# Two-layer recurrent model, one core: the first attention's maxima two heads at a time and evenly spaced between its scores, keys and values of the next layer in the score banks, and one written list behind it

## The chip, the cores and the metric

The kernel runs on one core of one Trainium2 chip. The metric is the device time of one execution in microseconds (us), the median of several runs. TensorE (PE) multiplies, VectorE (DVE), ScalarE (ACT) and GpSimd (POOL) work on elements, SyncE (SP) issues the transfers.

## The reference

```python
x = L0_attn_x                       # 1 x 1024 x 512, float32
xn = _layernorm(x)
s = _L0_attn_ref(xn, ...)           # 1024 tokens, 8 heads of width 8
g = _silu(_L0_ffn_ref(xn, ...))     # base 512x512, plus top-2 of 8 experts of rank 16
x = x + s * g
xn = _layernorm(x)
s = _L1_attn_ref(xn, ...)           # 32 query heads, 8 key/value heads of 128, rms-normed q and k, ALiBi, causal
g = _silu(_L1_ffn_ref(xn, ...))     # NF4 weights 1376x512 plus rank 16
x = x + s * g
```

In `_L0_attn_ref` the shapes come from the input, so it is attention of all 1024 tokens over all 1024 tokens, 8 heads of width 8, with biases in the projections. `_L1_attn_ref` is causal over 1024 tokens. All matrices are float32; the kernel multiplies each as a high and a low part, so that one product is three matmuls (`mm3`).

## The kernel before, in words

The 1024 tokens are `NT` = 8 blocks of 128, `D` = 512 is `KT` = 4 slices of 128. Each engine has its own program; semaphores tie them, and nothing but the order in which each program is written sets the order of the work. PSUM has eight banks: `T[0]` and `T[1]` (a ring of two), `S[0]` and `S[1]` (two banks each, scores), `VB`, `WB`.

**Front.** Layer norm, projections `qk`, values and router `var`, and from these the maxima of the scores of half unit 0: `max0(x)` for x = 0 to 15 (4 blocks of queries times 4 heads). PE writes 128x1024 scores of one head to `S[x % 2]` (L1936), DVE takes the maximum (L1430) into `MX`. PE may start `max0(x)` when the maximum x - 2 is done. Between them stand the other `qk`, and DVE computes the routing (`RT`, `CMP`, L1449 to L1488), from which POOL makes the expert weights `HN` (L905).

**First attention.** 32 steps x (`NBX`), that is 4 units u (two groups of 4 heads by two halves of queries) times 8 blocks of keys. `unit_items(x)` lists a step for all engines: `("ST", 0)`, `("ST", 1)` are the transposed scores of heads 0, 1 and of heads 2, 3 (`keys0`, L2021; each matmul uses the 32 rows of its head), exponentiated by ACT (L1095); `("PV", x-1)` are the values of the step before (`values0`, L2032, four column strips). In the steps up to 23, `("MM", u, j)` is one of 16 pairs of maxima of the next unit: two heads' scores into both banks of the ring `T` (`max1` on PE, L2005), two reductions on DVE (L1506). A pair may start when both banks are free. Pairs with even j use heads 2, 3 and so fit beside `("ST", 0)`, odd j beside `("ST", 1)`. `FILL` holds what runs between: `("B", t, kt)` the base product of a token block into `WB`, `("X", t)` the transposed `HN`, `("HN", t)` the experts' product, after which ACT empties `WB` (L1144). `("SH", u)` transposes the shifts into the ring and DVE adds them (L1992, L1520). From step 24 the first four blocks go on (`token_items`): `OS` sums transposed, DVE `normalise`, `OH` transposed heads, `WO` output product, DVE gate (L1561), POOL adds x (`add_x`, L943), `LS` statistics, POOL `rstd` (L845, L846), `LA` normalisation on DVE (L1361), `XT` transpose, ACT and DVE high and low parts.

**Tail.** Behind the last values stand `TAIL` = `tail_items(0)` to `tail_items(11)`: the same for blocks 4 to 7, and for the second layer keys and values of the eight blocks (`KV`, into the ring `T`; ACT squares L1206 and the high part of the values L1208; DVE copies L1662, L1663), POOL's inverse root (L867, L868), the scaling `SC` (L1669), the transposed keys `KT` (L2144, L1181, L1640), queries `PQ` into `WB` with `SQ` and `QT`, and the first scores `S0`. After the list 64 slots of the second layer follow, which the change leaves as they are.

Of the kernel before, what the change touches and what calls it, by code (L numbers as in the profile page):

```python
# [102 lines left out]
for _x in ([("F", t) for t in range(NT)] + [("WO", t) for t in range(EARLY)] + [("PQ", 0)] + [("WO", t) for t in range(EARLY, NT)] + [("PQ", 1)]):  # L103
# [35 lines left out]
def unit_items(x):  # L139

    maxima = [[pair(2 * x + PAIRS_PRE + i)] if 2 * x + PAIRS_PRE + i < 3 * PAIRS else [] for i in range(2)]
    a, b = (min(n, FILL_X) * len(FILL) // FILL_X for n in (x, x + 1))
    fill = FILL[a:b] + head_items(x - EARLY_X)
    seq = [("ST", 0)] + maxima[0]
    if x:
        seq.append(("PV", x - 1))
    if x in (7, 15, 23):
        seq.append(("SH", x // NT + 1))
    return seq + [("ST", 1)] + maxima[1] + fill
# [116 lines left out]
KV_STEP = (0, 0, 1, 2, 6, 7, 8, 10)  # L266
SC_STEP = (1, 1, 2, 3, 7, 8, 9, 11)
KT_STEP = (2, 3, 4, 5, 8, 9, 10, 11)
TAIL_STEPS = 12


def tail_items(k):


    seq = [("XT", EARLY - 1), ("KV", 0), ("PQ", 0)] if k == 0 else []
    seq += token_items(EARLY + k, EARLY, NT)
    if k == 9:
        seq.append(("PQ", 1))
    seq += [("SC", b) for b in range(NT) if SC_STEP[b] == k]
    if k == 11:  # L280
        seq.append(("SQ", 1))
    seq += [("KT", b) for b in range(NT) if KT_STEP[b] == k]
    seq += [("KV", b) for b in range(1, NT) if KV_STEP[b] == k]
    return seq + {1: [("SQ", 0)], 2: [("QT", 0)], 11: [("S0", 0), ("QT", 1)]}.get(k, [])


TAIL = [x for k in range(TAIL_STEPS) for x in tail_items(k)]
T_AT = {}
for _x in TAIL:
    if _x[0] in ("OS", "OH", "XT", "KT", "KV", "QT"):  # L290
        T_AT[_x] = T_OUT + len(T_AT)
# [124 lines left out]
def program(nc, x, w0, w1, codes, absmax, lora, consts, rows, rel, out):  # L416
    with ExitStack() as ctx:
# [36 lines left out]
        RSTD = sb("RSTD", [P, 2])  # L454
        SQK = sb("SQK", [P, 3, 8])
# [67 lines left out]
        hn_ready = sem("hn_ready")  # L523
        m_high = sem("m_high")
# [12 lines left out]
        k0_ready = sem("k0_ready")  # L537
# [7 lines left out]
        bo_high = sem("bo_high")  # L545
        bo_low = sem("bo_low")
# [52 lines left out]
        def y_psum(u):  # L599
# [4 lines left out]
            return S[a // 2][:, a % 2 * D:(a % 2 + 1) * D]  # L604

# [226 lines left out]
        def _(pool):  # L832
# [8 lines left out]
            def rstd(t):  # L841
# [4 lines left out]
                e.tensor_tensor(RSTD[:, k:k + 1], VE[:, k:k + 1], C[:, C_EXP:C_EXP + 1], ALU.pow).then_inc(rstd_ready, 1)  # L846
# [99 lines left out]
            for x in range(NBX):  # L946
# [4 lines left out]
                for it in unit_items(x):  # L951
                    if it[0] == "MM" and it[2] == PAIRS - 1:
# [9 lines left out]
            for k in range(TAIL_STEPS):  # L962
# [383 lines left out]
        def _(dve):  # L1346
# [1098 lines left out]
```

## Time and profile before

| | |
|---|---|
| median of 3 runs | 1472.75 us (1472.74 to 1473.64) |
| profiled execution, own time | 1472.16 us |
| its span in the trace | 1470.4 us |
| PE busy over the span | 1379.7 us (94%) |
| DVE, ACT, POOL busy | 986.7, 855.6, 634.0 us |
| granted clock of PE, mean | 0.983 of full |

Times in the trace count from the start of the span. The stages that the change touches end at 269.65 us, where the first slot of the second layer starts.

### The profile page before, as it was taken

How to read it: one execution, taken by the hardware profiler on the slowest of the kernel's cores; microseconds unless marked ns; L12 is line 12 of the kernel's file. 1: busy time of each engine (PE TensorE's matmuls, PEld its weight loads, DVE VectorE, ACT ScalarE, POOL GpSimd, SP SyncE). 2: the span in 40 equal slices, each digit the busy share in tenths (PEclk: the TensorE clock that was granted, in tenths of full speed). 3: DMA queues.
4: the chain of work that ended last, by engine and by line, in shares of the span. 5: the costliest groups of instructions: out<-in, count | busy, mean ns of one | idle time of the engine just before them, and what ended most of it. 6: DMA issues, size and time to landing. Idle time of an engine off the chain costs nothing.

```text
span 1470.4 us, 21362 instructions
## 1 busy us (share of the span) xinstructions
PE 1379.7 (94%) x7350; PEld 1082.0 (74%) x7350; DVE 986.7 (67%) x1852; ACT 855.6 (58%) x2105; POOL 634.0 (43%) x965
## 2 busy tenths in 40 slices
PE   4989987899999999999999999999999999989997
PEld 3733435688778888877888887888878877768786
DVE  6666656577677777678777777777687777675233
ACT  2335572566666666676666666676666666563211
POOL 4313263644344545445443555444444445433311
PEclk9979998999999999999999999999999999999999
DMA  4200022101020111002010101100020111113010
GB/s 141 65 1 1 1 77 77 37 8 45 15 73 21 40 35 39 30 30 73 1 60 13 61 21 39 59 15 31 30 73 1 45 35 38 37 58 134 15 58 29
DMA packets 35883, 61.02 MB, mean 41 GB/s; under 512 B 9056, under 2 KB 13280, under 8 KB 35776
## 3 DMA queue, kind: packets, MB, share of 16 engines
q1 hardware_dynamic: 35776, 59.66, 12.7%
q8 instruction: 59, 0.97, 0.3%
q14 instruction: 48, 0.39, 0.1%
HBM read 49.68 MB, written 9.96 MB: 41 GB/s over the span
## 4 chain that ended last, share of the span: by engine, by line
PE 66%; DVE 8%; issue 6%; ACT 1%; POOL 1%; DMA 0%; POOLq 0%; SPq 0%; DVEq 0%
PE T L2246 7%; PE T L1877 7%; PE T L1879 6%; PE T L1878 6%; PE S L1879 4%; PE S L1878 4%; PE S L1877 4%; PE VB L1879 4%; PE VB L1877 4%; PE WB L1877 4%; PE WB L1879 4%; PE WB L1878 4%; PE VB L1878 4%; PE T L2139 2%; DVE R L1654 2%
## 5 line engine op out<-in xcount | busy, mean ns | idle before, releaser
L852 POOL TENSOR_TENSOR RI<-SM,C 128x1 f32<-128x1 f32 x256 | 143.3, 560 | 503.2 <-ACT PB L1187 501.9
L1647 DVE CUSTOM_DVE_ANT_0 PB<-S,REL,SLC 128x128 f32<-128x128 f32 (+7 forms) x256 | 204.5, 813 | 78.3 <-PE S L1879 76.8
L1187 ACT ACTIVATE PB<-PB,NM 128x128 f32<-128x128 f32 (+7 forms) x256 | 198.8, 777 | 69.6 <-DVE NM L1647 64.7
L1251 ACT ACTIVATE R<-T 128x512 fp32r<-128x512 f32 x288 | 170.6, 593 | 100.5 <-PE T L2246 98.6
L853 POOL TENSOR_SCALAR PB<-PB,RI 128x128 f32<-128x128 f32 (+7 forms) x256 | 215.2, 840 | 25.2
L1654 DVE TENSOR_TENSOR R<-T,R 128x512 fp32r<-128x512 f32 x288 | 197.5, 688 | 42.1 <-ACT R L1251 23.7
L2246 PE MATMUL T<-C,PB 128*128 128x128 f32 x1152 | 176.6, 276 | 12.0 <-DVE R L1654 6.8
L2246 PEld LDWEIGHTS T<-C,PB 128*128 128x128 f32 x1152 | 134.1, 140 | 48.1 <-DVE R L1654 18.0
L1166 ACT ACTIVATE JUNK<-WB 128x128 bf16<-128x128 f32 x256 | 67.2, 277 | 92.8 <-PE WB L1879 92.8
L1877 PE MATMUL WB<-R,XT 128*128 128x512 f32 x288 | 116.6, 405 | 2.7 <-ACT G L1144 2.7
L1878 PE MATMUL WB<-R,XT 128*128 128x512 f32 x288 | 113.8, 395 | 0.0
L1879 PE MATMUL WB<-R,XT 128*128 128x512 f32 x288 | 113.7, 395 | 0.0
L1877 PE MATMUL T<-R 128*128 128x512 f32 x256 | 103.8, 406 | 3.9 <-issue 2.1
L1879 PE MATMUL T<-R 128*128 128x512 f32 x256 | 100.6, 393 | 0.0
L1878 PE MATMUL T<-R 128*128 128x512 f32 x256 | 100.0, 391 | 0.0
L1238 ACT ACTIVATE DQ<-DQ 128x704 f32<-128x704 int32 x128 | 97.2, 783 | 4.6 <-ACTq L1260 2.8
L1877 PE MATMUL S<-R 128*128 128x512 f32 (+3 forms) x252 | 93.5, 371 | 0.0
L1095 ACT ACTIVATE PB<-S 128x1024 f32<-128x1024 f32 x64 | 65.1, 1024 | 44.7 <-PE S L2021 44.7
L1879 PE MATMUL S<-R 128*128 128x512 f32 (+3 forms) x252 | 90.9, 361 | 0.0
L1728 DVE TENSOR_TENSOR DQ<-DQ 128x704 f32<-128x704 f32 x96 | 88.6, 923 | 0.0
L1506 DVE TENSOR_REDUCE MH<-T 128x1 f32<-128x512 f32 x96 | 61.9, 686 | 39.3 <-PE T L2005 39.3
L1877 PE MATMUL T<-R,XT 128*128 128x256 f32 x288 | 84.1, 292 | 3.4 <-DVE R L1640 1.7
(277 smaller groups left out, 3496.6 us busy)
## 6 DMA issues: line engine op xcount, KB each, us to landing
RAW<-w SPq DMA_DIRECT2D x86, 256.0 KB, 2.8
DQ<-codes SPq DMA_DIRECT2D x16, 352.0 KB, 3.5
DQ<-absmax SPq DMA_DIRECT2D x16, 352.0 KB, 3.0
dequantised<-DQ SPq DMA_DIRECT2D x16, 352.0 KB, 2.2
PB<-x SPq DMA_DIRECT2D x12, 256.0 KB, 3.3
PB<-dequantised SPq DMA_DIRECT2D x5, 512.0 KB, 4.7
PB<-x_scratch SPq DMA_DIRECT2D x8, 256.0 KB, 3.9
out<-PB SPq DMA_DIRECT2D x8, 256.0 KB, 2.0
```

The costliest lines, as they stand in the source:

```text
L852: ch.link(e.tensor_tensor(RI[:, k:k + 1], SM[:, k:k + 1], C[:, C_EXP + 5:C_EXP + 6], ALU.pow))
L853: e.tensor_scalar(pb(m, a, 0, L), pb(m, a, 0, L), RI[:, k:k + 1], scale, ALU.mult, ALU.mult).then_inc(probs_ready, 1)
L1187: e.activation(pb(m, a, 0, L), pb(m, a, 0, L), ACT.Exp, scale=-1.0, bias=NM[:, k:k + 1], accum_out=SM[:, k:k + 1]).then_inc(exp_done, 1)
L1238: e.activation(DQ[:, to, :], CODES, ACT.Copy, scale=sc, bias=bi).then_inc(line, 1)
L1251: e.activation(r(PT + AT[i, ("PV", kb)] % 3 * 1024, 512), T[AT[known, it] % 2][:, :], ACT.Copy).then_inc(t_act, 1)
L1647: e.tensor_tensor_reduce(out=pb(m, a, 0, L), in0=bank[:, 0:L], in1=REL[:, TOK - L:TOK], scale=SLC[:, a:a + 1], scalar=3.0e38, op0=ALU.add, ...
L1654: e.tensor_tensor(r(o + 512, 512), bank[:, :], rf(o, 512), ALU.subtract).then_inc(t_free, 1)
L1728: e.tensor_tensor(DQ[:, b, :], DQ[:, b, :], DQ[:, 3, :], op).then_inc(line_used, 1)
L1877: e.matmul(dst, lh, rh, start=start, stop=False)
L1878: e.matmul(dst, lh, rl, start=False, stop=False)
L1879: return e.matmul(dst, ll, rh, start=False, stop=stop)
L2246: last = e.transpose(bank[:, a * P:(a + 1) * P], pb(i, a, kb * P, (kb + 1) * P), IDENT)
```

## The change

**Front.** `max0` on PE now takes two heads at a time: four matmuls, alternating between the heads, into both of `S[0]` and `S[1]`, and starts when both maxima of the pair before are done. DVE's reductions keep their count. `qk(7)` on DVE moves behind the first shift, and only 4 of the 12 base matmuls of block 0 stand ahead of the shift.

**First attention.** The two pairs ahead of step 0 are gone. `couples(x)` places the 48 pairs: in each step one pair behind `("ST", 0)` and one behind `("ST", 1)`, and two of the fill items stand between the values and `("ST", 1)`. Steps 2 and 4 have a third pair, step 0 has one. The base product is cut in single matmuls, five fill matmuls a step. `HN` is transposed four blocks at a time, into `VB` ahead of step 0 (`turn_hn(0)`) and into `WB` at step 11 (`XB`), no longer through the ring. The first four blocks start at step 23, and all their items are done within the 32 steps.

**Tail.** One written list. Keys and values go to quarters of the `S` banks (`kv_psum`), the first queries to `VB`. DVE's copy of the keys is gone: `SC` scales from PSUM. The normalisation of blocks 4 to 7 moves from DVE to ACT (`apply_act`), for which POOL makes a bias in two further operations.

```diff
-FILL = [("X", 0), ("HN", 0)]
+BASE_PRE = 6
+_b = [("B", 0, m) for m in range(3 * KT)]
+FILL = {0: _b[BASE_PRE:10], 1: _b[10:] + [("HN", 0)], 11: [("XB", 0)]}
 for _t in range(1, NT):
-    FILL += [("B", _t, 0), ("B", _t, 1), ("X", _t), ("B", _t, 2), ("B", _t, 3), ("HN", _t)]
+    _b, _x = [("B", _t, m) for m in range(3 * KT)], 3 * _t - (1 if _t < EARLY else 0)
+    FILL.update({_x: _b[:5], _x + 1: _b[5:10], _x + 2: _b[10:] + [("HN", _t)]})
...
+    u, k = (1, x) if x < 7 else (x // NT + 1, x % NT)
+    if x == 0:
+        return None, ("MM", 1, 1), None
+    if x < 7:
+        even = k - 1 if k <= 2 else k
+        odd = k if k <= 4 else k + 1
+        return ("MM", 1, 2 * even), ("MM", 1, 2 * odd + 1), {2: ("MM", 1, 4), 4: ("MM", 1, 11)}.get(x)
+    if k == 7:
+        return ("MM", u, LAST), (("MM", u + 1, 1) if u < 3 else None), None
+    return ("MM", u, 2 * k), ("MM", u, 2 * k + 3), None
...
-EARLY_X = 24
+EARLY_X = 23
...
-    return seq + [("ST", 1)] + maxima[1] + fill
+    seq = [("ST", 0)] + ([first] if first else []) + ([("PV", x - 1)] if x else [])
+    seq += fill[:2] + [("ST", 1)] + ([second] if second else []) + fill[2:] + ([extra] if extra else [])
+    return seq + ([("SH", x // NT + 1)] if x in (7, 15, 23) else [])
...
-TAIL = [x for k in range(TAIL_STEPS) for x in tail_items(k)]
+TAIL = [("KV", 0), ("OS", 4), ("KV", 1), ("VL", 0), ("OH", 4), ("OS", 5), ("KV", 2), ("VL", 1), ("WO", 4),
...
+        ("VL", 6), ("SC", 6), ("KT", 6), ("S0", 0), ("VL", 7), ("SC", 7), ("KT", 7), ("SQ", 1), ("QT", 1)]
...
+def kv_bank(b):
+
+    return b % 2, b % 4 // 2 * 512
...
-            def max0(x):
-
-                qb, h = x // HEADS, x % HEADS
-                if x >= 2:
-                    pe.wait_ge(max_done, x - 1)
-                b = slice(h * 32, h * 32 + 32)
+            def max0(p):
+
+                qb, heads = p // 2, (p % 2 * 2, p % 2 * 2 + 1)
+                if p:
+                    pe.wait_ge(max_done, 2 * p)
                 for c in range(2):
...
+            def turn_hn(g):
+
+                if g == 1:
+                    pe.wait_ge(w_free, W_AT["XB", 0])
+                pe.wait_ge(hn_ready, 4 * g + 4)
...
+                if bias:
+
+                    ch.link(root)
+                    ch.link(e.tensor_tensor(NB[:, k:k + 1], MV[:, k, 0:1], RSTD[:, k:k + 1], ALU.mult))
+                    root = e.tensor_scalar(NB[:, k:k + 1], NB[:, k:k + 1], -1.0, 0.0, ALU.mult, ALU.add)
...
+            def apply_act(t):
...
+                e.activation(X1N[t], X1[t], ACT.Identity, bias=NB[:, k:k + 1], scale=RSTD[:, k:k + 1]).then_inc(xn_ready, 1)
```

PE's rows from the shift of unit 0 to the second half of step 0, before (T banks hold the shift and the maxima, `T<-C,DQ` is `HN` of one block):

```order
L1992 MATMUL T0<-C,L0S 128x128 x4
L2005 MATMUL T1<-R 128x512
L2005 MATMUL T0<-R 128x512
L2005 MATMUL T1<-R 128x512
L2005 MATMUL T0<-R 128x512
L2021 MATMUL S0<-R 128x512 x2
L2005 MATMUL T1<-R 128x512
L2005 MATMUL T0<-R 128x512
L2021 MATMUL S1<-R 128x512 x2
```

And after (`WB<-R,XT` L1980 are base matmuls, `VB<-C,DQ` is `HN` of four blocks):

```order
L2024 MATMUL T0<-C,L0S 128x128 x4
L1980 MATMUL WB<-R,XT 128x512 x2
L2076 MATMUL VB<-C,DQ 128x128 x4
L2053 MATMUL S0<-R 128x512 x2
L1980 MATMUL WB<-R,XT 128x512 x2
L2053 MATMUL S1<-R 128x512 x2
L2037 MATMUL T1<-R 128x512
L2037 MATMUL T0<-R 128x512
```

Two pairs of maxima ahead of the first scores are gone, and a third in step 0; base and `HN` matmuls stand there.

PE's rows of step 17, before (scores, maxima, values, scores, maxima, then the fill):

```order
L2021 MATMUL S0<-R 128x512 x2
L2005 MATMUL T1<-R 128x512
L2005 MATMUL T0<-R 128x512
L2032 MATMUL VB<-PB,L0S 32x512 x4
L2021 MATMUL S1<-R 128x512 x2
L2005 MATMUL T1<-R 128x512
L2005 MATMUL T0<-R 128x512
L1877 MATMUL WB<-R 128x512
L1878 MATMUL WB<-R 128x512
L1879 MATMUL WB<-R 128x512
L1877 MATMUL WB<-R,XT 128x512
L1878 MATMUL WB<-R,XT 128x512
```

And after, the same step:

```order
L2053 MATMUL S0<-R 128x512 x2
L2037 MATMUL T1<-R 128x512
L2037 MATMUL T0<-R 128x512
L2066 MATMUL VB<-PB,L0S 32x512 x4
L1980 MATMUL WB<-R,XT 128x512 x2
L2053 MATMUL S1<-R 128x512 x2
L2037 MATMUL T1<-R 128x512
L2037 MATMUL T0<-R 128x512
L1910 MATMUL WB<-R 128x512
L1911 MATMUL WB<-R 128x512
L1912 MATMUL WB<-R 128x512
```

Two fill matmuls stand between the values and the second scores, and the experts' product no longer has the next block's base product right behind it.

DVE's rows at the end of the tail, before (copy of keys, low values, scaling, queries, low keys, then the maxima of `S0`):

```order
L1662 COPY L0S<-T0 128x128
L1663 TENSOR_TENSOR R<-T0,R 128x128
L1669 TENSOR_SCALAR L0S<-L0S,SQK 128x128
L1623 TENSOR_TENSOR QN<-WB,INV 128x512
L1640 SCALAR_TENSOR_TENSOR R<-T1,QKW,R 128x128
L1647 ISA PB,NM<-S0,REL,SLC 128x128
```

And after:

```order
L1682 ISA PB,NM<-S1,REL,SLC 128x128
L1682 ISA NM 128x1
L1694 TENSOR_TENSOR R<-S1,R 128x128
L1704 TENSOR_SCALAR L0S<-S1,SQK 128x128
L1675 SCALAR_TENSOR_TENSOR R<-T0,QKW,R 128x128
L1658 TENSOR_TENSOR QN<-WB,INV 128x512
L1670 SCALAR_TENSOR_TENSOR R<-T1,QKW,R 128x512
```

The maxima of `S0` now stand ahead of the last key block, and the scaling of the second queries behind its low part.

## Rows read from the trace of the kernel before

**Rows 1.** Windows by stage: engines' busy us (count), granted clock, DMA share, GB/s

```profile
57.04:78.76 21.72, 21.67 (x90) 14.81 (x90) 17.83 (x32) 7.92 (x14) 5.18 (x7) 1.00 0.00 1
78.76:101.92 23.16, 17.37 (x64) 6.97 (x62) 12.09 (x19) 7.01 (x8) 4.13 (x8) 0.63 0.00 0
101.92:192.57 90.65, 83.59 (x452) 35.60 (x451) 56.81 (x94) 53.22 (x65) 24.59 (x27) 0.98 0.00 1
192.57:219.65 27.08, 24.25 (x141) 8.92 (x140) 14.71 (x35) 21.81 (x31) 22.13 (x23) 1.00 0.31 93
219.65:269.65 50.00, 37.24 (x196) 29.45 (x193) 28.01 (x81) 16.80 (x68) 21.23 (x39) 0.82 0.23 74
269.65:1470.40 1200.75, 1159.54 (x6244) 958.48 (x6242) 823.99 (x1524) 730.13 (x1888) 532.98 (x830) 0.99 0.12 39
```

**Rows 2.** Windows at one fall of the clock, in the middle

```profile
146.00:149.00 3.00, 3.00 (x9) 1.91 (x10) 1.58 (x3) 1.54 (x2) 0.00 (x0) 0.52 0.00 0
```

**Rows 3.** Timeline of PE in the front: start, us, operation [idle before]

```profile
54.76 0.73 PE L1936 MATMUL S<-R 32*128 32x512 f32 x2
...
57.04 0.73 PE L1936 MATMUL S<-R 32*128 32x512 f32 x2
...
60.65 0.73 PE L1936 MATMUL S<-R 32*128 32x512 f32 x4
61.31 0.50 PE L1877 MATMUL T<-XT,R 128*128 128x512 f32 x1
...
64.25 0.90 PE L1936 MATMUL S<-R 32*128 32x512 f32 x4
```

**Rows 4.** Timeline of DVE in the front, two maxima in a row

```profile
69.39 2.34 DVE L1430 TENSOR_REDUCE MX<-S 128x1 f32<-128x1024 f32 x2
```

**Rows 5.** Timeline of PE from the first shift to step 0

```profile
79.57 0.60 PE L1992 MATMUL T<-C,L0S 128*128 128x128 f32 x4
81.02 0.50 PE L2005 MATMUL T<-R 32*128 32x512 f32 x2 [0.85 <-DVE R L1520]
...
83.23 0.39 PE L2021 MATMUL S<-R 32*128 32x512 f32 x2
```

**Rows 6.** Timeline of PE in step 17

```profile
163.69 0.50 PE L2021 MATMUL S<-R 32*128 32x512 f32 x2
163.70 0.50 PE L2005 MATMUL T<-R 32*128 32x512 f32 x2
164.13 1.07 PE L2032 MATMUL VB<-PB,L0S 128*32 128x512 f32 x8
165.13 0.50 PE L2021 MATMUL S<-R 32*128 32x512 f32 x2
165.61 0.50 PE L2005 MATMUL T<-R 32*128 32x512 f32 x2
166.05 0.50 PE L1877 MATMUL WB<-R 128*128 128x512 f32 x1
```

**Rows 7.** Timeline of DVE, maxima of two following pairs

```profile
103.21 1.29 DVE L1506 TENSOR_REDUCE MH<-T 128x1 f32<-128x512 f32 x2 [0.58 <-PE T L2005]
105.08 1.29 DVE L1506 TENSOR_REDUCE MH<-T 128x1 f32<-128x512 f32 x2 [0.58 <-PE T L2005]
```

**Rows 8.** Timeline, steps 25 and 26: PE waits for ACT, ACT for a transfer

```profile
196.25 1.06 PE L2032 MATMUL VB<-PB,L0S 128*32 128x512 f32 x8 [0.97 <-ACT DQ L1120]
203.80 0.63 ACT L1125 ACTIVATE R<-RAW 128x512 fp32r<-128x512 f32 x1 [2.21 <-DMA RAW<-w]
```

**Rows 9.** Timeline in the tail, POOL and PE

```profile
244.43 1.26 POOL L943 TENSOR_TENSOR PB<-PB,G 128x512 f32<-128x512 f32 x1 [0.57 <-DVE G L1561]
245.77 0.25 POOL L845 TENSOR_SCALAR VE<-MV 128x1 f32<-128x1 f32 x1
246.10 0.55 POOL L846 TENSOR_TENSOR RSTD<-VE,C 128x1 f32<-128x1 f32 x1
265.94 0.48 PE L2144 MATMUL T<-C,L0S 128*128 128x128 f32 x1 [2.68 <-DVE L0S L1669]
```

More of the change, by code:

```diff
@@ L139, in unit_items @@
 def unit_items(x):
[L141 to L148, printed above, removed]
-    return seq + [("ST", 1)] + maxima[1] + fill
+    fill = FILL.get(x, []) + head_items(x - EARLY_X)
+    first, second, extra = couples(x) if x <= 23 else (None, None, None)
+    seq = [("ST", 0)] + ([first] if first else []) + ([("PV", x - 1)] if x else [])
+    seq += fill[:2] + [("ST", 1)] + ([second] if second else []) + fill[2:] + ([extra] if extra else [])
+    return seq + ([("SH", x // NT + 1)] if x in (7, 15, 23) else [])
 M_AT = {("SH", 0): 0}
 _k = 1
-for _i in [pair(n) for n in range(PAIRS_PRE)] + [i for x in range(NBX) for i in unit_items(x)]:
-    if _i[0] in ("MM", "SH", "X", "OS", "OH", "XT"):
+for _i in [i for x in range(NBX) for i in unit_items(x)]:
+    if _i[0] in ("MM", "SH", "OS", "OH", "XT"):
         M_AT[_i] = _k
@@ L1443, in _ @@
             var(0)
-            for t in range(1, NT):
+            var(1)
+            for t in range(2, NT):
+                max0(t - 2)
                 var(t)
-                if t < NT - 1:
-                    max0(t - 1)
             ch.settle()
@@ L1580, in _ @@
             add_shift(0)
-            for n in range(PAIRS_PRE):
-                max1(*pair(n)[1:])
+            qk(7, *QK_THEN[4])
+            low_hn(0)
             for x in range(NBX):
@@ L2076, in _ @@
             turn_shift(0)
-            for n in range(PAIRS_PRE):
-                max1(*pair(n)[1:])
+            for m in range(4, BASE_PRE):
+                base_part(0, m)
+            turn_hn(0)
             for x in range(NBX):
@@ L2115, in ring0, with project_q @@
                     pe.wait_ge(m_free, M_END)
-            def project_q(row, wait_w, chunk):
-                pe.wait_ge(w_free, wait_w)
+            def project_q(row, wait_w, chunk, bank=WB, full=w_full):
+                if wait_w is not None:
+                    pe.wait_ge(w_free, wait_w)
                 for kt in range(KT):
@@ L2122, in project_q, with project_kv @@
                     c = kt * 768
-                    last = mm3(WB[:, :], xt(0, kt, row * P, P), xt(1, kt, row * P, P), r(W_H + c, 512),
+                    last = mm3(bank[:, :], xt(0, kt, row * P, P), xt(1, kt, row * P, P), r(W_H + c, 512),
                                r(W_L + c, 512), kt == 0, kt == KT - 1)
-                last.then_inc(w_full, 1)
-            def project_kv(row, k, bank, chunk):
-                ring(k)
+                last.then_inc(full, 1)
+            def project_kv(row, k, bank, chunk, full=t_full):
+                if k is not None:
+                    ring(k)
                 pe.wait_ge(split, chunk + (QL1 + 1))
```

332 lines of the change are left out of this document (173 added, 159 removed), and 5 rows, old and new, of the table TAIL.

## The prediction

> **What bounds the kernel now.** I read the page first: PE is busy 94% of the span, so the whole is a question of what PE waits for, and at which clock it runs. The windows cut at the stages come next [rows 1]. The slots behind 269.65 us take 1200.75 us, and the change leaves them as they are; everything is decided in the 213 us between 57 and 270. There the stages differ. In the front PE is busy 21.67 of 21.72 us. From the shift to step 3 it is busy 17.37 of 23.16 us at a mean clock of 0.63, that is at 1.2 GHz most of the time. In steps 3 to 23 it is busy 83.59 of 90.65 us. In the last eight steps it is busy 24.25 of 27.08 us, and in the tail 37.24 of 50.00 us at a mean of 0.82. A share (1 - 0.82) x 2 = 0.36 of the tail, some 18 us, thus ran at the lower level; the reader is to see that a pause costs twice, once itself and once in what runs slowly behind it. In the middle one fall stands alone: from 146 to 149 us PE is busy all the time at 0.52 [rows 2], and 3 us at half speed lose 1.5 us.
>
> Then I read PE's timeline inside the stages. In step 17 the first scores and the first pair of maxima start 0.01 us apart and take 0.43 us together, up to the values; the values take 1.00 us; the second scores start at 165.13, but their pair only at 165.61, and the group takes 0.92 us instead of 0.43 [rows 6]. DVE's timeline says why: two reductions take 1.29 us, and 0.58 us pass until those of the next pair [rows 7]. A pair needs both banks of the ring, so pairs can follow each other only every 1.87 us, and in step 17 they are asked for 1.43 us apart.
>
> **The change part by part.** All sums are against the profiled execution's own 1472.16 us (span 1470.4 us); the median of the runs is 0.59 us above it. "Saves" is at full clock first; the clock gets a term of its own.
>
> **Front.** Before, one head and one `var` take 57.04 - 54.76 = 2.28 us [rows 3]. Two heads together take 0.66 us (60.65 to 61.31, the row of four matmuls) [rows 3]; in the later front neighbouring heads already ran like that, so only six times a saving is possible, at most 3 x 0.66 = 2.0 us. But PE now has to wait for both maxima of the pair before, and DVE has the second of them behind the copies of a `var`. I take 0.8 us. Behind it five rounds of one pair and one `qk` follow. PE needs 3.60 us for a round (60.65 to 64.25) [rows 3]. DVE needs 2.34 us for two maxima [rows 4], some 0.7 us for the join and up to 1.3 us for routing work; with the 0.7 us that the scores take, and no second pair in flight, rounds come to 3.6, 3.9, 4.2, 3.8 and 3.8 us. The last maximum is then 19.5 us behind the first of these rounds, and the shift 20.4 us, where it was 79.57 - 57.04 = 22.5 us [rows 3, 5], since 8 base matmuls are gone from ahead of it. Saved: 0.8 + 2.1 = 2.9 us. Bounds: nothing, and 5 us.
>
> **Shift to step 0.** Before 83.23 - 79.57 = 3.66 us, with two pairs of maxima in it [rows 5]. Now 0.6 us of transposes, two base matmuls (0.6), and the transposes of `HN` (0.6), for which POOL's first four products must be there: about 0.1 us of wait. That is 2.0 us, 1.7 us less. DVE's shift (0.7 us) is done by then.
>
> **Steps 0 to 23.** Before 192.57 - 83.23 = 109.3 us [rows 1, 5], in steps 3 to 23 90.65 / 21 = 4.32 us each. Now a step is: scores and maxima together 0.43, values 1.00, two fill matmuls 0.66, scores and maxima 0.43, three fill matmuls 0.89, sum 3.41 us. The fill is (3.60 - 0.66) / 12 = 0.245 us a matmul [rows 3] and some 0.16 us for each change to and from the small tiles. DVE allows a pair every 1.87 us [rows 7]. From the first to the second pair PE needs 2.09 us, so that leg is PE's; from the second to the next first it needs 1.32 us, so that leg is DVE's and takes 1.88. A step takes 3.97 us. What ends last is thus the ring again, and this is why only 0.35 us of the 0.91 us between 4.32 and 3.41 are got. Eighteen steps at 3.97 (71.5), two with a third pair at 3.97 + 1.88 (11.7), three with a shift at some 4.8, since DVE adds it ahead of the next scores (14.3), and 3.3 for step 0: 100.8 us, 8.5 us less. The pauses behind `G` (ACT empties `WB`) fall away, because the next base matmul now comes 1.4 us later, behind scores and values. The other end is 4.32 us a step as before.
>
> At this place the Trainium skill speaks against the change: TensorEngine Tiling (Array Packing), in Tiling Modes under Key Properties, says that a change of the tiling mode drains TensorE. The new order changes mode twice more in a step. By the rows a group of two small matmuls and the change behind it take 0.44 us (165.61 to 166.05), and I have charged 0.16 us for each further change. By a full drain, half a matmul's 0.50 us more each, the first leg would be 2.41 us, the step 4.29 us, and nothing would be saved here.
>
> **Steps 24 to 31 and the last values.** Before 27.08 us, 2.8 of them idle [rows 1]. One transpose of sums moves ahead (0.4), one `XT` comes in (0.5). Worse: `PV` of a step waits for the exponential of its second scores, 1.6 us behind them, and now the short items stand ahead of these scores. In steps 24, 27, 30 and 31 no PE work is behind them, and each waits 0.76 us where one waited 0.97 before [rows 8]. The transfer for which ACT waited 2.21 us [rows 8] stays as late, because POOL frees its buffer at the same time; I add 0.6 us. Cost 2 us, between 0 and 5.
>
> **Tail.** Its PE work at full clock is 37.24 less half of what ran slowly, about 30 us; that is the floor, 50.0 us the ceiling [rows 1]. I walked the new list with the durations of the timelines. Per block POOL has 1.26 us for x, 0.25 and 0.55 for the root [rows 9], and now two small operations more, some 0.55 us with their links; DVE has 0.6 us of normalisation less (ACT takes it, and is idle two thirds of the tail). With keys and values off the ring PE always has a projection of 1.5 us to put between the links of a chain. Four pauses remain: the ring slot of `XT` 4 behind `OH` 7, for which DVE first has statistics of block 5 (2.2 us); `QT` 0, whose root on POOL stands behind that of block 6 (1.1); `KT` 4 behind `QT` 0 on the ring (1.3); and the end, where squares, root, scaling, transpose, low keys and only then the second queries follow each other (with `S0` between, 3 us). At the end of the old list the same chain cost 2.68 us [rows 9]. Sum 37.8 us at full clock, 12.2 us less.
>
> **Clock.** The old times hold their own slow stretches, mine hold none. New pauses that could bring a fall: 1.6 us around the third pairs of steps 2 and 4, and the four of the tail. I charge 3 us for the steps (two falls like that of rows 2) and 2.5 us for the tail, where the pauses are further apart than the 5 us out of 12 of before.
>
> **Sum.** 2.9 + 1.7 + (8.5 - 3.0) - 2.0 + (12.2 - 2.5) = 17.8 us less: 1472.16 - 17.8 = 1454.4, and with the 0.6 us between this execution and the median, **1455 us**.
>
> **The rivals.**
>
> 1. *Everything holds at full clock.* The two charges for the clock go: 1449.5 us. For it: at 190 to 219 us pauses of up to 0.97 us left the clock at 1.00 [rows 1, 8]. Against: one fall came in the middle without a long pause [rows 2]. Chance 0.12.
> 2. *The gain of the even steps is lost.* Through the drain above, or because the step at 3.97 us is too thinly filled for full clock now and then: 5.5 us less gain plus some 2 us, 1462 us. For it: 4.32 us with PE at 92% had a fall already. Chance 0.17.
> 3. *The tail stays long.* Five ring users in a row behind a DVE that serves one list for four chains; each slip pauses PE, and the clock falls as it did. A tail of 45 us instead of 40.3: 1460 us; with 48, 1463. For it: a list has no slack where an estimate is wrong. Against: PE has 30 us of work for it. Chance 0.17.
> 4. *Slower.* PE idles 0.13 us in each leg that DVE ends and the small matmuls do not keep the granted clock up, so whole stretches run at 1.2 GHz, as from the shift to step 3 now [rows 1]. A step would then be PE's, 2 x 3.41 = 6.8 us, 2.8 more than at full clock. Beyond the charge, six further steps at the lower level use up the 17.8 us; from seven on it is slower than before, and with fifteen of the 24 it is 1497 us. Against: a step at half clock is busy without a pause, and the fall of rows 2 was over in 3 us. Chance 0.05.
>
> The forecast itself has 0.49.
>
> **How the numbers follow.** The forecast's own range is 1450 to 1459. Down to 1447 lies rival 1 with 2 us more from the front's bound; rivals 2 and 3 reach to 1463. Both at once and rival 4 are left out above: 1447 to 1464. A difference of 0.2% (3 us) is about what a measurement of this kernel tells from none. Faster by more than that is everything up to 1469.8: 0.92. Within it 0.03 (2 and 3 together with a bad clock), slower 0.05.
>
> **What would show it.** The first slot of the second layer starts at about 252 us instead of 269.65. The shift's transposes at 76.7; step 0 near 78.6; step 24 near 182; the last values end near 212. In a middle step both pairs start within 0.05 us of their scores or 0.56 us behind them alternately, and pairs on DVE come every 2.09 and 1.88 us. The tail takes 40 us, with a granted clock above 0.9. The prediction is wrong if step lengths stay at 4.3, if the clock between 79 and 182 us averages below 0.9, or if the tail takes over 44 us; and if the slots behind it take more than 1 us longer than 1200.75, something that I have not seen is behind it.

## The result, and the profile after

The changed kernel takes **1467.66 us** (median of 13 runs, 1462.94 to 1471.58). The kernel before, timed beside it, takes 1473.32 us (13 runs, 1468.53 to 1474.0). The ratio is 0.9963, 95% interval 0.9954 to 0.9971: faster by 0.37%, where the prediction had 1.2%. 1467.66 lies 3.7 us above the range. The profiled execution took 1465.94 us, its span is 1464.0 us.

Windows of the kernel after, cut at the starts of step 0, step 8, step 16 and step 24, at the end of the last values, at the first slot and at the `QT` items of slots 0 and 1; the last row is all slots (columns as in [rows 1]; the granted clock is the number behind POOL's count).

```profile
78.59:115.77 37.18, 32.15 (x167) 12.35 (x166) 23.74 (x38) 19.15 (x22) 7.57 (x11) 0.95 0.00 1
115.77:155.13 39.36, 34.45 (x171) 12.90 (x172) 22.73 (x35) 19.45 (x23) 11.30 (x12) 0.87 0.00 1
155.13:188.18 33.05, 31.59 (x174) 12.51 (x174) 21.35 (x36) 19.86 (x24) 9.52 (x10) 1.00 0.00 0
188.18:217.19 29.01, 23.70 (x142) 8.71 (x143) 15.97 (x33) 21.64 (x30) 21.09 (x23) 1.00 0.32 95
217.19:260.73 43.54, 34.44 (x192) 28.39 (x189) 21.09 (x67) 19.04 (x72) 23.42 (x51) 0.83 0.24 79
260.73:275.75 15.02, 12.84 (x54) 10.27 (x53) 7.55 (x13) 7.40 (x20) 5.81 (x10) 0.83 0.00 0
275.75:296.45 20.70, 19.72 (x107) 16.22 (x107) 13.42 (x27) 13.48 (x38) 10.87 (x19) 0.92 0.17 52
260.73:1464.00 1203.27, 1162.35 (x6244) 960.60 (x6242) 824.67 (x1524) 730.04 (x1886) 531.12 (x826) 0.99 0.12 39
```

The same two slots in the kernel before:

```profile
269.65:283.48 13.83, 11.65 (x54) 9.44 (x52) 7.55 (x13) 7.78 (x22) 7.23 (x14) 0.90 0.00 0
283.48:302.62 19.14, 18.18 (x106) 15.03 (x107) 13.38 (x27) 13.49 (x38) 11.17 (x19) 1.00 0.19 57
```

Set side by side, in us, each a difference of starts in the two traces (57.04 is the same time in both, step 0 starts at 83.23 before and 78.59 after):

| stretch | before | after | change | predicted |
|---|---|---|---|---|
| front, 57.04 to the shift's transposes | 22.53 | 19.67 | -2.9 | -2.9 |
| shift to step 0 | 3.66 | 1.88 | -1.8 | -1.7 |
| steps 0 to 23 | 109.34 | 109.59 | +0.2 | -5.5 |
| steps 24 to 31, last values | 27.08 | 29.01 | +1.9 | +2.0 |
| tail | 50.00 | 43.54 | -6.5 | -9.7 |
| slots | 1200.75 | 1203.27 | +2.5 | 0 |

Three of the six terms hold within 0.1 us; the steps miss by 5.8 us, the tail by 3.2, the slots by 2.5. Next, the longer pauses of PE in its timeline of the kernel after:

```profile
91.49 0.50 PE L2037 MATMUL T<-R 32*128 32x512 f32 x2 [1.37 <-DVE MH L1540]
132.85 0.79 PE L2037 MATMUL T<-R 32*128 32x512 f32 x2 [1.94 <-DVE MH L1540]
153.72 0.63 PE L2024 MATMUL T<-C,L0S 128*128 128x128 f32 x4 [1.46 <-POOL L0S L945]
192.28 1.07 PE L2066 MATMUL VB<-PB,L0S 128*32 128x512 f32 x8 [1.69 <-ACT DQ L1147]
231.02 1.12 PE L1931 MATMUL T<-C,PB 128*128 128x128 f32 x4 [1.48 <-DVE R L1588]
```

At 132.85 the duration of the pair's matmul is 0.79 instead of 0.50 us: PE is at the lower of its two levels, 1.2 GHz. The window of the next 11 us, whose mean granted clock is 0.54, and DVE's timeline just ahead:

```profile
133.00:143.90 10.90, 10.90 (x40) 3.73 (x40) 4.35 (x7) 3.08 (x4) 0.00 (x0) 0.54 0.00 0
```

```profile
128.68 1.29 DVE L1540 TENSOR_REDUCE MH<-T 128x1 f32<-128x512 f32 x2 [0.58 <-PE T L2037]
130.91 0.69 DVE L1560 TENSOR_TENSOR R<-WB,R 128x512 fp32r<-128x512 f32 x1 [0.94 <-ACT R L1131]
131.51 1.28 DVE L1540 TENSOR_REDUCE MH<-T 128x1 f32<-128x512 f32 x2
```

At step 11 the low part of the four transposed `HN` (L1560) stands in DVE's list ahead of the second pair's maxima, and has to wait for ACT's high part. The maxima, whose scores PE had written by 130.7, start at 131.51; the ring stays full, and PE stands for 1.94 us. This is no accident of one execution: every trace in which the item stands at that place and step 10 is as in the changed kernel (the changed kernel's and four of the experiments') has the 1.94 us and the fall behind it.

### The profile page after: what moved, and what is told of

Read it like the earlier page. It is cut to its first block, busy times and chain, and to the rows that moved or that the text cites. A ratio compares the mean times of both kernels' runs of the same rounds, so it can differ in the third digit from the quotient of the medians.

```text
span 1464.0 us, 21333 instructions
## 1 busy us (share of the span) xinstructions
PE 1373.5 (94%) x7350; PEld 1076.4 (74%) x7350; DVE 981.1 (67%) x1834; ACT 855.6 (58%) x2103; POOL 634.2 (43%) x973
## 4 chain that ended last, share of the span: by engine, by line
PE 75%; DVE 12%; issue 7%; ACT 3%; POOL 2%; DMA 1%; POOLq 0%; DVEq 0%; SPq 0%; ACTq 0%
PE T L2298 7%; PE T L1910 7%; PE T L1912 6%; PE T L1911 6%; PE S L1912 5%; PE S L1911 5%; PE S L1910 5%; PE WB L1910 4%; PE VB L1912 4%; PE VB L1910 4%; PE WB L1911 4%; PE WB L1912 4%; PE VB L1911 4%; PE VB L2066 2%; PE T L2181 2%
## 5 line engine op out<-in xcount | busy, mean ns | idle before, releaser
L1910 PE MATMUL WB<-R,XT 128*128 128x512 f32 x252 | 100.4, 398 | 0.0
L1911 PE MATMUL WB<-R,XT 128*128 128x512 f32 x252 | 99.6, 395 | 0.0
L1912 PE MATMUL WB<-R,XT 128*128 128x512 f32 x252 | 99.5, 395 | 0.0
L1910 PE MATMUL S<-R 128*128 128x512 f32 (+3 forms) x252 | 93.1, 370 | 0.9 <-DVE NM L1682 0.9
L1912 PE MATMUL S<-R 128*128 128x512 f32 (+3 forms) x252 | 90.5, 359 | 0.0
L1911 PE MATMUL S<-R 128*128 128x512 f32 (+3 forms) x240 | 86.0, 358 | 0.0
```

Source lines behind the costliest of these rows:

```text
L1910: e.matmul(dst, lh, rh, start=start, stop=False)
L1911: e.matmul(dst, lh, rl, start=False, stop=False)
L1912: return e.matmul(dst, ll, rh, start=False, stop=stop)
```

## The experiments

My theory after the result: the pauses that the new order leaves (at the third pairs, at step 11, at the shift of step 15, in the tail) are what keeps the clock falling, and with them gone most of the missing 11.5 us comes back. Each run below is timed against the kernel before on the chip that it ran on, and these were three chips. A difference to the changed kernel "by ratios" is the difference of the two ratios, times 1473 us; "by medians" it is the bare difference, which also holds what the chips differ by. Each trace is of one execution.

### HN of step 11 behind the second pair

```diff
-    seq += fill[:2] + [("ST", 1)] + ([second] if second else []) + fill[2:] + ([extra] if extra else [])
+    cut = 0 if x == 11 else 2
+    seq += fill[:cut] + [("ST", 1)] + ([second] if second else []) + fill[cut:] + ([extra] if extra else [])
```

> The changed kernel with one item moved: in step 11 the transposed HN of blocks 4 to 7 stands behind the second pair of maxima instead of ahead of the second scores. My theory (pauses that the new order leaves are what keeps the granted clock falling): DVE's low part no longer stands ahead of the second pair's reductions, the pause of 1.94 us before 132.85 goes, and the 10 us at half clock behind it (133 to 143) go too. Step 16 starts near 150 instead of 155.1, and the time falls by 3 to 6 us. Rival (only the pause itself costs, the clock falls anyway somewhere near): 1 to 2 us less, with a fall of the same length elsewhere between 125 and 150. Rival (nothing depends on it, DVE's ring is the bound): within 0.5 us.

Measured: 1461.84 us (6 runs), ratio 0.9937 (0.9920 to 0.9954): 3.8 us less than the changed kernel by ratios, whose intervals just touch, and 5.8 by medians. Steps 8 to 15 in its trace, and its tail, which the edit does not concern:

```profile
116.69:151.21 34.52, 31.11 (x172) 12.11 (x173) 22.70 (x35) 19.45 (x23) 11.29 (x12) 1.00 0.00 1
213.25:254.25 41.00, 31.45 (x193) 26.05 (x189) 21.05 (x67) 18.89 (x72) 22.83 (x49) 0.94 0.25 83
```

34.52 instead of 39.36 us, at full clock: pause and fall went together, and the time with them, 4.8 us. Step 16 starts at 151.21. The size is well founded: with the item in its old place the same eight steps take 39.20 to 39.36 us in four traces (the changed kernel's, the fillers', the moved statistics' and the last eight steps'), and 37.83 us with POOL's gate moved, at a clock of 0.86 or 0.87 each time; with the gate and the item both moved, in the combined kernel below, they take 33.01, which is 4.8 us less again. The tail is another matter. Its list is untouched here and takes 41.00 us, against 43.54 in the changed kernel's trace; over the seven traces with this list and no fillers it takes 41.0 to 43.5 us, at clocks of 0.83 to 0.94. A difference of 2.5 us in the tail of a single trace shows nothing by itself.

### POOL's gate of block 3 behind its shift

```diff
                     if it[0] == "MM" and it[2] == LAST:
                         shift0(it[1])
+                        if x == 15:
+                            gate0(3)
                     elif it[0] == "HN":
                         add_bias0(it[1])
-                        if it[1]:
+                        if it[1] and it[1] != 4:
                             gate0(it[1] - 1)
```

> The changed kernel with POOL's gate of block 3 moved behind its shift of step 15. Theory: TensorE's transposes of that shift no longer wait 1.46 us at 153.72; step 16 starts 1.4 us earlier, and everything behind it too; the clock is 1.00 around it before and after. Expected 1.2 to 1.6 us less. Rival: the transposes then wait for something else that is due at the same time, for DVE's reductions: under 0.5 us.

Measured: 1464.68 us (12 runs, 1459.22 to 1476.84), ratio 0.9953 (0.9933 to 0.9972). The pause of 1.46 us is gone from the timeline, but so wide a spread does not separate it from the changed kernel's 0.9963 (1.5 us by ratios). The stage shows it: steps 8 to 15 take 37.83 us in its trace against 39.36, and in the combined kernel below 33.01 against 34.52 with the first edit alone, so it is worth 1.5 us, as expected. Over the twelve runs the time follows the mean granted clock, from 1459.22 us at 0.989 to 1476.84 us at 0.974. The profiled execution, the slowest of the twelve, shows one thing that the spread is made of. Windows of its steps 16 to 23, and of a stretch behind the same pause that is at 192.28 above:

```profile
157.30:190.34 33.04, 31.59 (x172) 12.53 (x172) 21.35 (x36) 19.86 (x24) 10.13 (x11) 1.00 0.00 0
194.44:226.31 31.87, 29.64 (x104) 10.01 (x104) 13.74 (x28) 16.96 (x24) 18.19 (x20) 0.57 0.21 67
```

```profile
194.44 1.87 PE L2068 MATMUL VB<-PB,L0S 128*32 128x512 f32 x8 [1.69 <-ACT DQ L1149]
...
211.24 1.60 PE L2068 MATMUL VB<-PB,L0S 128*32 128x512 f32 x8 [1.11 <-ACT PB L1125]
```

The same 1.69 us in front of the same instruction: no fall in the changed kernel's execution, 32 us at a mean of 0.57 in this one. It is two falls, with some 3 us at full speed between them; the second begins behind the 1.11 us at 211.24, which the changed kernel has too (at 203.09) and passes at full speed.

### More fill in the steps with a third pair

```diff
+_seq = [i for x in range(2, 11) for i in FILL[x]]
+_n = {2: 8, 3: 5, 4: 8, 5: 4, 6: 4, 7: 4, 8: 3, 9: 3}
+_at = 0
+for _x in range(2, 11):
+    _w = _n.get(_x, 99)
+    FILL[_x] = _seq[_at:_at + _w]
+    _at += len(FILL[_x])
```

> The changed kernel with the same fill matmuls dealt out differently: eight in steps 2 and 4, where a third pair stands, and four or three in steps 5 to 9. Theory: the pauses of 1.37 us before 91.49 and of 1.15 us before 102.90 shrink by 0.7 us each, and the fall of the clock at 92 to 95 us goes; step 8 starts at 114 instead of 115.8, 1.5 to 2.5 us less in all. Rival (thinner steps 5 to 9 lower the clock): step 8 near 116 or later, and the time the same or up to 3 us more.

Measured: 1466.96 us (12 runs, 1461.11 to 1475.43), ratio 0.9968 (0.9953 to 0.9982): no difference from the changed kernel. The two short pauses ahead of the third pairs went, but those of 1.36 and 1.14 us behind them stayed, since three pairs in a step need the ring for 3 x 1.88 us wherever the fill stands. Windows of steps 0 to 7, 8 to 15 and 16 to 23:

```profile
77.78:115.07 37.29, 32.12 (x173) 13.27 (x172) 23.73 (x38) 19.90 (x23) 10.74 (x13) 1.00 0.00 1
115.07:152.61 37.54, 31.89 (x166) 11.99 (x166) 22.73 (x35) 18.94 (x22) 8.13 (x9) 0.85 0.00 1
152.61:187.75 35.14, 33.76 (x173) 13.17 (x174) 21.35 (x36) 19.97 (x24) 9.53 (x10) 0.91 0.00 0
```

In steps 0 to 7 the fall did go, and the clock was 1.00, but they took 37.29 us, no less than the 37.18 us at 0.95 in the changed kernel's trace (other traces with the old fill have 37.21 to 40.86). The thinner steps have waits of their own, as the 0.69 us for `WB` at 107.88. The fall in steps 8 to 15 is not new, since the changed kernel has one there too (39.36 us at 0.87); here it begins behind a pause of 1.15 us in step 11, and the edit's list had run out before step 10, which was left without any fill (the edit's numbers for steps 2 to 9 sum to all 39 items). The fall in steps 16 to 23 begins behind POOL's gate ahead of the shift, behind which five traces of the even order with about the same 1.46 us have none. So step 8 started no earlier for the full clock, which is what the rival said, and the timed runs show no gain. Whether the edit or chance gave the later falls, one trace cannot say.

### Matmuls in the tail's pauses

```diff
+            FILLER = {('KT', 0): 4, ('XT', 4): 6, ('KT', 4): 5, ('KT', 7): 4, ('QT', 1): 7}
+            def filler(n):
+                for _ in range(n):
+                    e.matmul(VB[:, 0:P], IDENT, IDENT, start=True, stop=True)
```

> The changed kernel with 26 further matmuls of 128 columns, of the identity with itself, into a bank that nobody reads then, placed in five pauses of the tail (4, 6, 5, 4 and 7 of them, some 0.2 us each). Their result is not used. Theory (the clock falls behind the pauses, and slots 0 and 1 lose 2.75 us through the low clock that the end of the tail hands on): the waits stay, but the granted clock in the tail rises from 0.84 to over 0.95; the tail takes 40 to 41 us instead of 43.5, and the slots up to 296 us 1.5 to 2.75 us less: 4 to 6 us less in all. Rival (the tail's list and its chains over DVE are what costs): the tail's end stays within 1 us of 260.7 or comes later by the fillers' own time, and the whole changes by less than 1.5 us.

Measured: 1464.22 us (6 runs), ratio 0.9939 (0.9924 to 0.9955). Windows of its tail and of slots 0 and 1:

```profile
218.14:260.04 41.90, 38.14 (x244) 33.70 (x241) 21.09 (x67) 19.00 (x72) 24.18 (x52) 0.92 0.26 82
260.04:272.64 12.60, 10.41 (x56) 8.50 (x54) 7.55 (x13) 7.40 (x20) 5.08 (x8) 1.00 0.00 0
272.64:293.35 20.71, 19.75 (x107) 16.19 (x107) 13.33 (x27) 13.49 (x38) 11.25 (x19) 0.92 0.17 52
```

Slot 0 is 2.4 us shorter, at full clock, and that is the fillers' doing: without them it takes 14.7 to 15.0 us in all seven traces with this list. Slot 1 got nothing back. The tail's 41.90 us lie within the 41.0 to 43.5 that the list takes without fillers, so that they shortened it is not shown, and its clock stayed under the 0.95 that I expected. In all it is 3.5 us by ratios and 3.4 by medians, a little under the 4 to 6 expected, and the interval overlaps the changed kernel's.

### All fill behind the second pair

```diff
-    seq += fill[:2] + [("ST", 1)] + ([second] if second else []) + fill[2:] + ([extra] if extra else [])
+    seq += [("ST", 1)] + ([second] if second else []) + fill + ([extra] if extra else [])
```

> The changed kernel with all fill items of a step behind the second pair, so that the pairs are spaced unevenly again. If the even spacing is what shortened the step (the change's own sum), the pause of 0.44 us in front of the second pair's maxima comes back and the step of 4.01 us grows to 4.3 or more: 7 us more over the steps, about 1475 us. If it is the number of fill matmuls and not their place, PE's legs are 1.43 and 1.82 us at full clock, both under DVE's 1.88, and a step is 3.76 to 4.0 us: within 5 us less and 1 us more than the changed kernel. The low part at step 11 stands ahead of the second pair in neither, so its pause of 1.94 us should be gone here as in the first experiment.

Measured: **1455.59 us** (4 runs, 1453.02 to 1457.06), ratio 0.9873 (0.9845 to 0.9902): 13 us less than the changed kernel by ratios, 12 by medians, with intervals well apart. Three things are in it: the spacing of the steps, the item of step 11, which now stands behind the second pair too, and the last eight steps. PE's timeline over one middle step of the changed kernel:

```profile
158.56 0.49 PE L2053 MATMUL S<-R 32*128 32x512 f32 x2
159.14 0.50 PE L2037 MATMUL T<-R 32*128 32x512 f32 x2
159.57 1.07 PE L2066 MATMUL VB<-PB,L0S 128*32 128x512 f32 x8
160.57 0.73 PE L1980 MATMUL WB<-R,XT 128*128 128x512 f32 x2
161.23 0.50 PE L2053 MATMUL S<-R 32*128 32x512 f32 x2
161.24 0.50 PE L2037 MATMUL T<-R 32*128 32x512 f32 x2
161.67 0.50 PE L1910 MATMUL WB<-R 128*128 128x512 f32 x1
...
162.56 0.50 PE L2053 MATMUL S<-R 32*128 32x512 f32 x2
163.15 0.49 PE L2037 MATMUL T<-R 32*128 32x512 f32 x2
```

And of the uneven kernel:

```profile
160.89 0.49 PE L2053 MATMUL S<-R 32*128 32x512 f32 x2
160.98 0.50 PE L2037 MATMUL T<-R 32*128 32x512 f32 x2
161.41 1.07 PE L2066 MATMUL VB<-PB,L0S 128*32 128x512 f32 x8
162.41 0.50 PE L2053 MATMUL S<-R 32*128 32x512 f32 x2
162.85 0.50 PE L2037 MATMUL T<-R 32*128 32x512 f32 x2
163.28 1.42 PE L1980 MATMUL WB<-R,XT 128*128 128x512 f32 x5
164.63 0.49 PE L2053 MATMUL S<-R 32*128 32x512 f32 x2
164.73 0.50 PE L2037 MATMUL T<-R 32*128 32x512 f32 x2
```

Pairs start at 160.98, 162.85 and 164.73: 1.87 and 1.88 us apart, both at DVE's pace, a step of 3.75 us. In the even order the leg from 159.14 to 161.24 takes 2.10 us, which is PE's, and the other 1.91, so a step takes 4.00 us. The pause of 0.44 us ahead of the second pair is back, and costs nothing, since DVE does not wait for it. Spacing by PE's work made one leg longer than DVE needs and saved nothing in the other. Steps 16 to 23 show the sum of it with both at full clock: 31.22 us in the best kernel further below against 33.05 in the changed one, and the other edits of that kernel do not touch these steps.

### The uneven order in the last eight steps alone, and in the steps with maxima alone

The cut is `2 if x <= 23 else 0` in the first and `0 if x <= 23 else 2` in the second.

> The changed kernel with the fill behind the second scores in steps 24 to 31 alone. Theory (the short items that stand ahead of the second scores make the values wait for their exponential): the 29.0 us from step 24 to the end of the values become 27.0, as in the uneven kernel; about 2 us less than the changed kernel, and the falls of the clock in the steps as before. Rival (the gain of the uneven order is all in the steps with maxima): within 0.5 us of the changed kernel.

> The changed kernel with the fill behind the second pair in steps 0 to 23 alone; the transposed HN of step 11 is then behind the second pair too. Theory: a plain step takes 3.75 us instead of 4.01, which is 4 to 5 us over the steps, and the pause and fall at step 11 go, 4 to 6 us: step 24 near 181 instead of 188.2 and 8 to 10 us less in all than the changed kernel. Rival (the low clock that the uneven order has at 90 to 100 and 148 to 154 us eats it up): 4 to 6 us less, what the first experiment gave for step 11 alone.

Measured: 1463.98 us (6 runs), ratio 0.9949 (0.9932 to 0.9967), whose interval overlaps the changed kernel's; and 1457.16 us (5 runs), ratio 0.9899 (0.9884 to 0.9913), 9.4 us less than the changed kernel by ratios (10.5 by medians), as expected. In the windows steps 24 to 31 take 27.14 us in the first, as expected, and 29.00 in the second; step 24 starts at 181.42 in the second. So most of the gain is in the steps with maxima: 2.1 and 9.4 us by ratios (3.7 and 10.5 by medians). The 9.4 us still hold the item of step 11. Against the first experiment, which has that out of the way (0.9937), 5.6 us are left to the spacing itself, and these two intervals lie apart.

### One item of the tail's list moved

```diff
-("KT", 0), ("LA", 4), ("LS", 5), ("WO", 6), ("OH", 7), ("SC", 2)
+("KT", 0), ("LA", 4), ("WO", 6), ("OH", 7), ("LS", 5), ("SC", 2)
```

> The changed kernel with one item of the tail's list moved: the statistics of block 5 stand behind the low part of OH 7 instead of ahead of it. Theory (DVE's one list serves four chains and PE waits at the ring for an item that needs nothing from the statistics): the pause of 1.48 to 1.93 us before XT 4 shrinks under 0.5 us, and with it the fall of the clock behind it (228 to 235): the tail 1.5 to 4 us shorter. Rival (XT 4's own chain, the normalisation of block 4, is due at the same time): the pause stays over 1 us, with another releaser, and nothing is gained.

Measured: 1463.97 us (6 runs), ratio 0.9932 (0.9905 to 0.9959). PE's pause before `XT` 4 is 0.68 instead of 1.48 us, but the profiled tail is only 0.6 us shorter, still at a clock of 0.83; the 1.5 to 4 us that I expected are not in it. Slots 0 and 1 take 13.62 and 19.13 us in this trace instead of 15.02 and 20.70, which the theory did not have. The time is 4.6 us lower by ratios and 3.7 by medians, and the intervals overlap.

### Three edits together

The first, the second and the fillers (nine ahead of `XT` 4).

> The changed kernel with the three edits that went the theory's way: HN of blocks 4 to 7 behind the second pair of step 11, POOL's gate 3 behind its shift, and fillers in five pauses of the tail (29 of them, nine ahead of XT 4). If the gains are separate they add up: 5.8 us from the first, 1.4 from the second, and 3 to 4 from the fillers, with slot 0 at full clock: 1455 to 1457 us. If a fall of the clock that is taken away in one place comes back in another (rival), no more than the first edit's gain is left: 1460 to 1462 us.

Measured: 1456.49 us (6 runs, 1452.49 to 1463.41), ratio 0.9888 (0.9858 to 0.9918), within the sum (11 us less than the changed kernel). The profiled execution is the slowest of the six; its steps 24 to 31 had a fall as the one above and took 39.70 us at 0.66. Its tail ran at full clock:

```profile
221.40:260.45 39.05, 35.90 (x250) 31.20 (x247) 21.07 (x67) 18.90 (x72) 22.47 (x49) 1.00 0.26 86
```

39.05 us lie under the 41.0 to 43.5 of the list without fillers.

### The kernel before, with fillers in its own tail

Nine pauses, 43 matmuls: `OH` 4 and 5 three each, `OS` 7, `WO` 6 and 7 two each, `XT` 5 nine, `KT` 4 three, `KV` 7 seven, `KT` 7 twelve.

> The kernel before, with 43 matmuls of the identity with itself in nine pauses of its own tail, into a bank that nobody reads then. It tells how much of the tail's 50.0 us was the clock and how much the old list. If the new list's gain is mostly its order, the old tail stays at 48 us or more with fillers. If the clock was the larger part, it comes down to 44 to 46 us, and slot 0 from 13.8 to 12.6 us: 5 to 7 us less in all, which is as much as the whole change gave.

Measured: 1469.31 us (12 runs), ratio 0.9972 (0.9956 to 0.9988), 4 us less than the kernel before, where I expected 5 to 7. Its clock is 1.00 through the tail, and the tail takes 46.6 us (221.0 to 267.61), slot 0 12.57 us. That lies between my two cases for the tail, 44 to 46 and 48 or more. So of the old tail's 50.0 us 3.4 were the clock, if one trace of each stands for the rest; the new list, both with fillers and at full clock, is 7.5 us shorter (39.05). That is the list with all that changed in it: the order, the copy that is gone, and the normalisation on ACT. The three were not tried apart.

### The best of it

> Uneven fill in all steps, POOL's gate 3 behind its shift, statistics of block 5 behind the low part of OH 7; no fillers. If the parts add up to the 1455.6 us of the uneven kernel: 1.4 us less for the shift and 0.5 to 3 us for the tail, 1451 to 1454 us. If a fall of the clock only changes place, 1455 to 1456 us.

> The same with 23 fillers in five pauses of the tail. The tail at full clock took 39.05 us with fillers against 41.0 to 43.5 without, and slot 0 12.6 against 15.0: 3 to 5 us less than without fillers, 1447 to 1450 us. Rival (the low clock comes back behind, in slot 1 or in the steps 24 to 31): less than 2 us.

Measured: **1447.09 us** without fillers (4 runs, 1445.91 to 1448.39), ratio 0.9827 (0.9813 to 0.9840), and 1445.96 us with them (4 runs), ratio 0.9819 (0.9805 to 0.9832), not told apart. The first is the change with three moves of written order and no added work, and beats both kernels: 20 us less than the changed one by ratios. Its windows, steps 8 to 15, 16 to 23, 24 to 31, tail, slots 0 and 1:

```profile
114.93:146.16 31.23, 30.10 (x171) 13.34 (x171) 22.07 (x35) 19.91 (x23) 10.98 (x12) 1.00 0.00 1
146.16:177.38 31.22, 30.41 (x172) 13.76 (x172) 21.44 (x36) 20.47 (x24) 10.23 (x11) 1.00 0.00 1
177.38:204.40 27.02, 24.36 (x143) 9.07 (x143) 15.78 (x33) 21.59 (x30) 20.97 (x23) 1.00 0.30 94
204.40:242.92 38.52, 30.00 (x192) 24.97 (x189) 21.23 (x68) 19.05 (x72) 23.04 (x49) 0.95 0.28 95
242.92:256.90 13.98, 11.80 (x54) 9.55 (x52) 7.55 (x13) 7.40 (x20) 6.32 (x11) 0.89 0.00 0
256.90:276.00 19.10, 18.11 (x106) 15.03 (x107) 13.29 (x27) 13.58 (x38) 11.14 (x19) 1.00 0.20 57
```

I had expected 1451 to 1454; steps 8 to 23 lost not only the shift's pause but every fall, and the tail came out at 38.52 us where the same list took 42.91 in the trace of the moved statistics. Why its clock was 0.95 here and 0.83 there stays open. With fillers slot 0 was 1.4 us shorter, but the tail 0.8 and slot 1 1.6 us longer (39.27 us at 0.96, 20.70 at 0.92): the gain changed place, as the rival had it.

## Why the prediction was wrong

**Front, shift, steps 24 to 31.** Right. The shift's transposes start at 76.71 (76.7 predicted), step 0 at 78.59 (78.6). The rounds of the front begin at 56.19 and take 3.64, 4.04, 4.26 and 3.84 us, where the prediction had 56.2 and 3.6, 3.9, 4.2 and 3.8, so the reason was right and not the sum alone. Steps 24 to 31 cost 1.9 us (2). That cost was not due, though: with the fill behind the second scores it is 27.0 us, no more than before.

**Steps 0 to 23: the step that failed.** The sum for this stage, "Eighteen steps at 3.97 (71.5), two with a third pair at 3.97 + 1.88 (11.7), three with a shift at some 4.8", has every other step as a plain one. Two items that occur once, and stand in another engine's way, were put at nothing: the transposed `HN` of step 11, whose low part stands on DVE ahead of the second pair's maxima, and POOL's gate ahead of the shift of step 15. The diff named `("XB", 0)` at step 11, and the prediction never asked what stands behind it on DVE. The first item costs 4.8 us with its pause and its fall (39.36 to 34.52 us, first experiment), the second 1.5 us. The sum, 100.8 us at full clock, came out at 109.6. The other 2.5 us of the 8.8 are 1.5 in steps 0 to 7, at a clock of 0.95, and about 0.4 in each of the two other groups. The charge of 3 us for the clock paid for some of it, and 5.8 are missing.

**The even spacing: a right number with a wrong reason.** "A step takes 3.97 us" is right (4.00), and so are its legs, 2.09 and 1.88 (2.10 and 1.91). But the prediction takes the spacing for what shortens the step, and it does the opposite. "What ends last is thus the ring again" holds for one leg only, and I never worked the same items out in the uneven order. By my own figures that is 0.43 + 1.00 for the first leg and 1.82 for the second, both under DVE's 1.88: 3.76 us a step, and 3.75 were measured. The even order loses 0.25 us a step to it. The error began with the reading of the kernel before. The pause of 0.48 us ahead of step 17's second pair [rows 6] was taken for the loss, but the leg across it is 1.91 us, DVE's own. Its trace shows where the length was. Over three steps, from 163.70 to 176.56, the six legs from pair to pair are 1.91, 2.99, 1.90, 1.88, 1.88 and 2.30 us. Two are over DVE's pace, and these rows stand in them:

```profile
167.70 0.50 PE L1877 MATMUL WB<-R,XT 128*128 128x512 f32 x1 [0.69 <-ACT G L1144]
175.54 0.33 PE L2041 MATMUL T<-C,DQ 128*128 128x128 f32 x1 [0.78 <-DVE MH L1506]
```

In the first leg stand six fill matmuls, and a wait until ACT has emptied `WB`; in the other the transposed `HN` takes a place in the ring. The change ended both: a step now has at most five fill matmuls, its next base matmul comes later, and the `HN` no longer pass the ring. That is read from one trace each; no run took the three apart. This error alone would have left the forecast standing.

**Changes of mode.** By the order of the rows the new step changes the tiling mode once more than the old one, not twice: base matmuls now stand between the values and the second scores. Splitting the five fill matmuls in two groups costs 0.66 + 0.89 - 1.35 = 0.20 us (160.57 to 161.23 and 161.67 to 162.56 in the even step, 163.28 to 164.63 in the uneven one), where 0.16 was charged. The rule of the Trainium skill (TensorEngine Tiling (Array Packing), Tiling Modes) is that a change of mode drains TensorE. The trace has no row for a drain; it shows that the leg, for which I had estimated 2.41 us by a full drain, took 2.10.

**Tail.** The new list is 7.5 us shorter than the old where both ran at full clock with fillers (46.6 and 39.05 us). The full-clock sum of 37.8 us was 1.3 short of 39.05, part of which may be the fillers' own time. The charge of 2.5 us for the clock was too small: 43.54 less 39.05 is 4.5. Some of that is this one execution, since the same list took 41.0 us in others. What failed is "the pauses are further apart". The prediction had four pauses; the trace has nine of 0.5 us or more in 43.5 us, and the kernel before had nine in 50.0, so they are no further apart, and the mean clock is 0.83, where it was 0.82.

**Slots.** That "the change leaves them as they are" is wrong by 2.5 us, and of the signs that the prediction named for being wrong this is the one that came (the clock of steps 0 to 23 was 0.94 and the tail 43.54 us, just inside their bounds). Slot 0 runs at 0.83 instead of 0.90, slot 1 at 0.92 instead of 1.00, with the same instructions and the same pause of 2.18 us for `QN` ahead of `QT`. For slot 0 the cause is the low clock that the end of the tail hands on: when the fillers keep the clock up, it takes 12.60 us. For slot 1 it is open, since it took 20.71 us at 0.92 behind that slot 0 at full clock too.

**Rivals.** Two of them came together in size: the gain of the steps was lost, and the tail stayed long. I had each at 0.17 and left the pair out of the range, though both hang on one clock. For the steps the reason was not the rival's, neither a drain nor a step too thinly filled, so that its price of 7.5 us lies near the 5.8 is luck. My theory after the result held in part. Removing the pauses at step 11 and at step 15 paid; in the tail only the gain in slot 0 is clear; spreading fill over those of the third pairs did not pay, and the even order itself, worth as much as the item of step 11, was not in the theory. It was found by undoing it.

## What to carry to other kernels

Where two engines alternate on a ring, work out both legs for each order of the same items: a step is the sum over the legs of the longer engine, so filler belongs where the ring's other engine is the slower, and even spacing is worth nothing for itself. Items that occur once (a conversion, a gate) need a look at each engine's list: what stands directly behind them, and who waits for that. A low clock is no local cost: charge the stage behind as well, and treat the losses of several stages as one risk. And compare a stage over several traces before a difference in it is put down to an edit.

## What the runs showed of the hardware

The same kernel with the same pauses does not fall in clock at the same places each time. Behind the pause of 1.94 us at step 11 there was a fall in all five executions traced with it, and none at that place in the first experiment, where the pause was gone. Behind the one of 1.69 us in step 24 there was no fall in the changed kernel's execution, and 32 us at a mean of 0.57 in another. Twelve runs of one kernel spread from 1459.22 to 1476.84 us, and the time followed the mean granted clock. The kernel with the three moves spread from 1445.91 to 1448.39 us, though in four runs only. Why a fall comes or not at the same pause stays open; no run here settles it. That added matmuls which nobody reads shorten a stage (the old tail from 50.0 to 46.6 us) I had expected. That they pay almost nothing in the best kernel (1.1 us, within the noise), I had not: there the 1.4 us that slot 0 gained were lost in the tail and in slot 1.
